# The gate products of the experts move from VectorE to GpSimd, in a fused attention and mixture-of-experts kernel

## What is computed

```python
h_NM2H = jnp.einsum('md,ndh->nmh', x_MD, Wl1) + bl1[:, None, :]
a_NMH, b_NMH = (h_NM2H[..., :H], h_NM2H[..., H:])
y_NMD = jnp.einsum('nmh,nhd->nmd', jax.nn.silu(a_NMH) * b_NMH, Wl2) + bl2[:, None, :]
```

## Time and profile before

| what | value |
|---|---|
| median of 3 runs | 1487.48 us (1483.25 to 1488.9) |
| the profiled execution | 1480.89 us, of which its span is 1479.3 us |
| busy, share of the span | PE 92%, DVE 87%, ACT 56%, POOL 53% |
| expert pairs, by TensorE | from 389.5 to about 1192.5 us of the span |
| end stage | from there to the end |

### The profile page before, as it was taken

How to read it: one execution, slowest core, us unless ns; L and a number is a source line. 1 busy time by engine, 2 the same in 40 slices (tenths; PEclk the granted TensorE clock), 3 DMA queues, 4 the chain that set the end, 5 groups by cost and what they waited for, 6 DMA issues and landing times.

```text
span 1479.3 us, 35888 instructions
## 1 busy us (share of the span) xinstructions
PE 1366.1 (92%) x13687; PEld 1088.9 (74%) x13688; DVE 1279.8 (87%) x1504; ACT 825.3 (56%) x1889; POOL 789.6 (53%) x566
## 2 busy tenths in 40 slices
PE   5998999986799999999999899999999887898997
PEld 4864565655688888888888788888888766676675
DVE  7837655565999999999999999999999999999961
ACT  2547678775555555556554445555554436675555
POOL 1001377774687676768667777758576631311111
PEclk9998899997999999999999999999999989898899
DMA  7943356777557676767766566767667568999797
GB/s 231 343 146 91 120 184 208 220 256 244 174 135 235 165 218 156 238 182 218 208 176 197 138 216 171 220 170 219 191 167 234 134 154 236 264 225 260 204 246 145
DMA packets 204250, 293.53 MB, mean 198 GB/s; under 512 B 25601, under 2 KB 161029, under 8 KB 203891
## 3 DMA queue, kind: packets, MB, share of 16 engines
q0 software_dynamic: 65792, 146.59, 38.1%
q1 hardware_dynamic: 135683, 144.84, 31.7%
q10 hardware_dynamic: 2672, 0.83, 0.2%
HBM read 182.83 MB, written 117.74 MB: 203 GB/s over the span
## 4 chain that ended last, share of the span: by engine, by line
PE 45%; DVE 39%; issue 6%; DMA 4%; SPq 3%; ACT 1%; POOL 0%; POOLq 0%; ACTq 0%; DVEq 0%
DVE gslope L1682 9%; DVE parts L1678 9%; PE pQK L657 8%; PE pY L1486 7%; PE pA L1480 7%; PE pB L1480 7%; DVE parts L1638 5%; PE pS L644 4%; PE pS L677 3%; DVE expert_mem L1604 3%; PE pOff L689 3%; SPq L1158 2%; DMA band<-band_rows 2%; DVE parts L1650 2%; PE pB L1514 1%
## 5 line engine op out<-in xcount | busy, mean ns | idle before, releaser
L1209 POOL DMA_INDIRECT moe_rows<-expert_mem,token_of x142 | 331.6, 2335 | 82.9 <-issue 50.9
L1480 PE MATMUL pA<-xsT,expert_mem 128*128 128x256 f32 x1136 | 261.7, 384 | 12.8 <-DMA expert_mem<-in_w_l 8.3
L1486 PE MATMUL pY<-expert_mem 128*128 x1136 | 267.0, 389 | 0.0
L1480 PE MATMUL pB<-xsT,expert_mem 128*128 128x256 f32 x1136 | 256.8, 379 | 0.0
L1480 PEld LDWEIGHTS pA<-xsT,expert_mem 128*128 128x128 f32 x1136 | 218.8, 193 | 44.3 <-issue 11.0
L1486 PEld LDWEIGHTS pY<-expert_mem 128*128 128x128 f32 x1136 | 212.0, 192 | 42.8 <-issue 16.3
L1480 PEld LDWEIGHTS pB<-xsT,expert_mem 128*128 128x128 f32 x1136 | 215.8, 190 | 29.3
L1190 POOL DMA_INDIRECT expert_mem<-xn_rows,token_of x138 | 194.7, 1411 | 71.9 <-issue 69.1
L1678 DVE SCALAR_TENSOR_TENSOR parts<-pos_pair,prob 128x768 f32<-128x768 f32 x256 | 227.8, 951 | 1.1
L1682 DVE TENSOR_REDUCE gslope<-parts 128x256 f32<-128x3072 f32 x64 | 214.7, 3354 | 2.2
L1329 ACT ACTIVATE expert_mem<-pA,b1sel 128x256 f32<-128x256 f32 x284 | 111.3, 474 | 134.5 <-issue 90.5
(11 more groups left out here) (199 smaller groups left out, 2049.7 us busy)
## 6 DMA issues: line engine op xcount, KB each, us to landing
expert_mem<-in_w_l POOLq DMA_DIRECT2D x71, 1024.0 KB, 6.8
band<-band_rows SPq DMA_DIRECT2D x256, 96.0 KB, 4.8
S_rows<-expert_mem SPq DMA_DIRECT2D x64, 376.0 KB
band_rows<-wgt SPq DMA_DIRECT2D x12, 1536.0 KB, 7.1
pos_pair<-pos_rows SPq DMA_DIRECT2D x28, 384.0 KB, 8.0
xn_rows<-expert_mem SPq DMA_DIRECT2D x16, 512.0 KB, 5.7
v_rows<-expert_mem SPq DMA_DIRECT2D x16, 512.0 KB, 4.6
moe_rows<-zeros POOLq DMA_DIRECT2D x4, 2048.0 KB
```

What stands on the lines that cost most here:

```text
L1209: nc.gpsimd.indirect_dma_start(out=dram["moe"], out_offset=bass.IndirectOffsetOnAxis(ap=keep["inv"][:, 2 * n + s:2 * n + s + 1], axis=0), ...
L1480: mm = nc.tensor.matmul(dst[:, c], w1[:, 1 - u, k, o * HID + c * P:o * HID + (c + 1) * P], xsT[:, k], start=(k == 0), stop=(k == KC - 1))
L1486: mm = nc.tensor.matmul(pY[:, s], hid[:, h, c, s * P:(s + 1) * P], w2[:, c, ds(e * D, D)], start=False, stop=(s == 1 and c == HC - 1))
```

## The change

The gate product of pair n-1 is made by GpSimd, in the routine of pair n, between the loads of rows and the scatters, instead of by VectorE between the parts of its steps. The instruction is the same `tensor_tensor` on the same tiles, with the same two waits in front and the same semaphore behind. The table of places and VectorE's calls go away. No buffer changes.

```diff
-GATES_AT = ((1, 2, 4, 5, 6), (0, 1, 3, 4, 5, 7), (0, 1, 3, 4, 6, 7), (0, 2, 3, 5, 6, 8), (0, 2, 4, 5, 6), (0, 1, 3, 4, 5, 7),
...
+            def gate_hidden(n):
+
+                pool.wait_ge(a_ready, n + 1)
+                pool.wait_ge(b_ready, n + 1)
+                h = n % HSLOTS
+                nc.gpsimd.tensor_tensor(hid[:, h], hid[:, h], act_a[:, h % 2], ALU.mult).then_inc(hid_ready, 1)
+
             def pair_io(n, u, first=False, left=SLOT_PAIRS):
...
                     load_xs(n + 2, u)
+                if n > 0:
+                    gate_hidden(n - 1)
                 if n >= LAG + 1:
                     take_y(n - LAG - 1, 1 - u)
...
-            def gate_hidden(n, h):
-
-                dve.wait_ge(a_ready, n + 1)
-                dve.wait_ge(b_ready, n + 1)
-                V.tensor_tensor(hid[:, h], hid[:, h], act_a[:, h % 2], ALU.mult).then_inc(hid_ready, 1)
-
...
                 def also(place):
-                    for n, h in dict(gates).get(place, ()):
-                        gate_hidden(n, h)
                     for k in dict(units).get(place, ()):
                         finish_unit(k)
...
-            scores(0, opening, lambda place: gate_hidden(0, 0))
-            gate_hidden(1, 1)
-            gated, unit = 2, 0
+            scores(0, opening)
+            unit = 0
             for it in range(STEPS):
-                gates, units = {}, {}
-                for place in GATES_AT[it] if it < len(GATES_AT) else ():
-                    gates[PLACES[place]] = [(gated, gated % HSLOTS)]
-                    gated += 1
```

More of the change, by code:

```diff
@@ L118 @@
 PLACES = ("half products", "products", "half scores", "scores", "weights 0", "weights 1", "weights 2", "weights 3", "end")
-GATES_AT = ((1, 2, 4, 5, 6), (0, 1, 3, 4, 5, 7), (0, 1, 3, 4, 6, 7), (0, 2, 3, 5, 6, 8), (0, 2, 4, 5, 6), (0, 1, 3, 4, 5, 7),
-            (0, 1, 3, 4, 6, 7), (0, 2, 3, 4, 6, 7), (0, 2, 4, 5, 6, 8), (1, 3, 4, 5, 7), (0, 1, 3, 4, 6, 7), (0, 2, 3, 4, 6, 7))
 EXPONENT_AFTER = (2, 8, 14, 20, 26, 31, 37, 43, 49, 54, 60, 66)
@@ L1697, in finish_tile, with step @@
                 V.tensor_tensor(here, here, moe[:, LAST % MOE_SLOTS, t % GROUP], ALU.mult).then_inc(out_ready, 1)
-            def step(it, chain_at, gates=(), units=(), first=False, last=False):
+            def step(it, chain_at, units=(), first=False, last=False):
                 chain = Chain(dve, chain_sem, chain_at)
                 def also(place):
-                    for n, h in dict(gates).get(place, ()):
-                        gate_hidden(n, h)
                     for k in dict(units).get(place, ()):
@@ L1754, in _ @@
             opening(products(0, range(BLOCK_KNOTS)))
-            scores(0, opening, lambda place: gate_hidden(0, 0))
-            gate_hidden(1, 1)
-            gated, unit = 2, 0
+            scores(0, opening)
+            unit = 0
             for it in range(STEPS):
-                gates, units = {}, {}
-                for place in GATES_AT[it] if it < len(GATES_AT) else ():
-                    gates[PLACES[place]] = [(gated, gated % HSLOTS)]
-                    gated += 1
+                units = {}
                 for place, some in UNITS_AT[max(it - BY_SP + 1, 0)].items():
@@ L1765, in _ @@
                     unit += some
-                step(it, it * CHAIN, gates=gates, units=units, first=it == 0, last=it == LAST)
-            assert gated == SLOT_PAIRS
+                step(it, it * CHAIN, units=units, first=it == 0, last=it == LAST)
             for k in range(unit, LAST):
```

## The result

The changed kernel takes 1523.5 us (median of 4 runs, 1520.6 to 1527.9) against 1487.5 us before: a ratio of 1.0257 (95% interval 1.0237 to 1.0277), 36 us slower. The profiled execution has a span of 1522.9 us, 43.6 more than before.

A forecast was written before the change was run, and what follows sets the result against it. TensorE and VectorE were both full; with the product GpSimd, at 12.5 us a pair, was to become the bound. 1480.9 + 84 - 5 - 5 = 1555 us, put at 1558 for a typical run (+4.7%), range 1495 to 1660.

The forecast's parts named there:

- GpSimd's need of a pair, 12.5 us: GpSimd's routine per pair: 9.3 us before plus 3.2 us for product, issue and wait, against TensorE's 11.31 us.
- The term +84 us: Over the 71 pairs, GpSimd as the bound adds 71 x (12.5 - 11.31) = +84 us.
- What it takes from VectorE: VectorE's step sheds products to 60.5 us, then gains six holds of 1.7 us: 70.7 us against 75 us of pairs.
- The first rival, VectorE held off: GpSimd's transfers wait less, need 11.7 us; VectorE's 70.7 us step rules: 1520 us; 1500 to 1530 us, chance 0.16.
- The 1563 us: VectorE held off in full at every product, a step of 74.3 us: +87 - 5, 1563 us.
- Where the lateness shows: GpSimd's late `w1` load makes TensorE wait for weights ahead of `pA`, about 1.2 us a pair.
- The sign that was named for this case: In the profile after, TensorE waiting while GpSimd waits too would mean VectorE and the exponents rule.
- The 5 us at the end and the 5 us of old stalls: VectorE's lead saves 5 us in the end stage (bounds 0 and 22); TensorE's present stalls, 5 us, go.
- no change: Product at 1.5 us and shorter waits: GpSimd needs 11.2 us a pair and fits; 1481 us, within 7; chance 0.09.
- faster: Product runs largely beside GpSimd's transfers and VectorE is relieved: 1470 us, -0.7%; chance 0.08.
- the dearer product: GpSimd's product of 2.7 us and a wait of 1.2 make 13.5 us a pair: 1626 us; above 1590, chance 0.15.
- the case that had a chance of 0.52: GpSimd's routine as the bound of the pairs, 1530 to 1590 us, chance 0.52.

The follow-up runs named there:

- the memsets: Changed kernel with two GpSimd memsets over both operands in place of the gate product: 1483.2 us, ratio 0.9993.
- the one-input instruction: Changed kernel with GpSimd multiplying b by 1.0 (one input, one output) in place of the gate product: 1502.6 us, ratio 1.0113.
- the other two places of the product in the routine: Changed kernel with the product behind the scatters (1745.8 us, ratio 1.0656) or between weights' load and gathers (1730.0 us, 1.058), on a chip at 1635.9 us before.

## Why the prediction was right in sign and range, and wrong in the bound

**What bounds the kernel**: right. TensorE at 11.31 us a pair and VectorE at 67 us a step were both full, and GpSimd's reserve was what the trace showed: the longer routine used it up.

**The product's duration**: right, 2.36 us for 2.3 (bounds 1.5 and 2.7). The estimate of 2.25 us, half of the 4497 ns of the Trainium skill, page "GPSIMD Engine Reference", section "Performance versus the Vector engine", agrees within 5%.

**GpSimd's need of a pair, 12.5 us**: this is the step that failed. In the beat, six routines take 69.4 us, 11.6 each; over the whole window it is 685.3 / 58 = 11.8, and that is the need at most, since GpSimd's waits for VectorE are in it. The 0.3 us of issue ahead of the product don't exist (it starts as the gather ends, 620.04 against 620.02), and its own wait for VectorE is 2.61 - 2.36 = 0.25 us for 0.6. These 0.65 us are small, but they decide which of two near limits comes first: 12.5 x 6 = 75 us against VectorE's 70.7 had made GpSimd the bound, 11.8 x 6 = 70.8 leaves them level, and the kernel with one scatter, whose routine is shorter by some 2 us, is no faster. The term +84 us measured +41; pairs of 12.5 us were 845.5 / 71 = 11.9.

**What it takes from VectorE**: right. The hold of 1.7 us measured 1.63, the step of 70.7 us measured 70.5, the own work of 60.5 us showed in the run without the product. This was put down as slack and was the bound. The first rival, VectorE held off, had 1520 us with a chance of 0.16, and the changed kernel takes 1523.5. It had been turned down because "75 is above both", a comparison of two estimates 6% apart that were not known so well. Its other reason, a VectorE that is full with no wait at all, was the better evidence: a full engine takes any hold at once, GpSimd's reserve of 2 us had to be used up first.

The rule of the Trainium skill, page "SBUF — State Buffer", section "SBUF: two separate sides", an exclusive lock between GpSimd and two-input instructions of VectorE, now has both directions in the trace, and its exception for GpSimd instructions that don't read (the memsets' 0.0 us) as well. The 1563 us that the prediction put to it, a full hold at every product, are too much, because a quarter of the products fell in a reduce and held nothing. And "for the whole instruction" isn't what the one-input instruction does, which held VectorE 1.0 us of its 2.82.

**Where the lateness shows**: wrong. TensorE was to wait for weights, 1.2 us a pair; it waited 7.6 us in all for them and 29.5 us behind ScalarE, which waited for VectorE. The sign that was named for this case, TensorE waiting while GpSimd waits too, came only by half: GpSimd had next to no waits. And VectorE, which was to be idle a few per cent, was never idle.

**The 5 us at the end and the 5 us of old stalls**: neither is there. From the thirteenth maximum to the last weights both kernels take 232 to 234 us. With no slack VectorE won no lead, so the bounds of 0 and 22 us were right and 0 was the value.

**Rivals**: no change and faster are excluded by the run; the dearer product didn't come, though the other two places of the product in the routine come near it (1582 and 1597 us for its 1626).

**The number**: 1523.5 us lies in the stated range from 1495 to 1660 us, but outside the 1530 to 1590 us of the case that had a chance of 0.52; the range held it because it took in the rival. The forecast itself was 34 us too high. Its last step has a slip, too: 1555 us and 0.4% are 1561, not 1558.

## What to carry to other kernels

Before work goes from VectorE to GpSimd, count VectorE's instructions with two SBUF inputs: in this kernel a GpSimd product of 2.36 us that met one held it off for 1.7 to 3.5 us, on the mean of all products 1.6 us for 1.14 us shed, so the exchange loses though the engine named idle was idle. Ask first what the relief is worth by leaving the work out altogether (here nothing, because ScalarE's places and TensorE's pairs set the pace). And where two limits come out within some 6% of each other, weigh the rival by which engine has no reserve, and not by the larger estimate.

## What the runs showed of the hardware that was not expected

- A one-input TENSOR_SCALAR of 128 x 1024 float32 took 2.82 us on GpSimd, the two-input TENSOR_TENSOR 2.36, and yet it held VectorE only about 1.0 us of that (0.68 on the mean). Two memsets of the same size took 0.97 us each and held nothing.
- The same GpSimd product took 2.36 us behind a gather, 2.90 behind a scatter and up to 2.98 behind a load of weights, because it started up to 0.6 us before the transfer ahead of it had ended; VectorE was held for this longer time, 3.4 us where its own instruction had begun just before.
- Engines that keep each other off can fall into a beat, 69.4 us or 70.1 us for step after step. A GpSimd routine with one scatter less, without such a beat, made the kernel slower (1539.8 for 1523.5 us), and VectorE with 3.5 us a step less to do won only 0.4 us of it (70.1 for 70.5).
- GpSimd's gathers and scatters waited for VectorE's two-input instructions (the scatters that met the sum of 5376 columns took 6.10 and 5.34 us, one alone 1.6). The load of weights, a plain transfer, took 0.75 to 1.42 us at every one of its 69 places in the kernel before.
